# One step of statistics moved from VectorE to TensorE and ScalarE in a kernel that normalises, shifts and blurs images

## What is computed

```
out = displace(group_norm(x, groups of 12 channels, eps 1e-5), round(offset))
kern = exp(-(dx*dx + dy*dy) / (2 * 0.5**2)), 3 x 3, made of frac = offset - round(offset), sum 1
result = x + depthwise_conv(out, kern)
```

## Time and profile before

| | us |
|---|---|
| median of 3 runs | 970.71 (970.06 to 973.06) |
| the profiled execution | 969.36 |
| its span in the profile | 967.6 |
| VectorE busy | 871.9 (90%) |
| ScalarE busy | 714.3 (74%) |
| GpSimd busy | 327.9 (34%) |
| TensorE busy | 201.3 (21%) |
| moved by DMA | 403.49 MB, mean 417 GB/s |

### The profile page before, as it was taken

The page is one execution under the profiler, slowest core; times in us unless marked ns, Lnnn a source line. Parts: engine busy times, 40 slices in busy tenths (PEclk is TensorE's granted clock), DMA queues, the critical chain, the costliest instruction groups (busy, mean ns, idle before and its releaser), DMA issues.

```text
span 967.6 us, 3646 instructions
## 1 busy us (share of the span) xinstructions
PE 201.3 (21%) x896; PEld 195.9 (20%) x896; DVE 871.9 (90%) x947; ACT 714.3 (74%) x412; POOL 327.9 (34%) x197
## 2 busy tenths in 40 slices
PE   0321312212122121222202212122122122220220
PEld 0321312212122121222202212112122122220220
DVE  6389899999999999899989999999999979669991
ACT  3998959777597777778677777777768787877730
POOL 4033341434424333333325264162522323123320
DMA  8999999999999999999999999999999999999997
GB/s 362 429 375 429 423 417 430 420 414 430 417 426 429 421 425 420 427 418 428 417 416 418 420 406 415 424 414 425 423 423 420 427 426 429 427 425 421 414 432 321
DMA packets 28234, 403.49 MB, mean 417 GB/s; under 512 B 3506, under 2 KB 3506, under 8 KB 3634
## 3 DMA queue, kind: packets, MB, share of 16 engines
q0 software_dynamic: 27648, 402.67, 99.4%
q1 hardware_dynamic: 562, 0.57, 0.2%
HBM read 201.90 MB, written 201.33 MB: 417 GB/s over the span
## 4 chain that ended last, share of the span: by engine, by line
DMA 45%; DVE 42%; issue 5%; ACT 4%; POOL 3%; SPq 0%; ACTq 0%; DVEq 0%; POOLq 0%
DMA out<-tiles,row_of 36%; DVE tiles L467 15%; DMA tiles<-x,row_of 8%; DVE rowblur L442 7%; DVE tiles L469 7%; DVE rowblur L447 7%; DVE normed L426 4%; POOL tiles L194 3%; ACT unread L259 3%; ACT unread L263 1%; DMA row_of<-rows 0%; DVE scale L381 0%; DVE shift L384 0%; POOL out L199 0%; DVE var_p L371 0%
## 5 line engine op out<-in xcount | busy, mean ns | idle before, releaser
L259 ACT ACTIVATE unread<-tiles 128x4096 uint8<-128x4096 f32 x94 | 339.9, 3616 | 150.4 <-DMA tiles<-x,row_of 149.8
L263 ACT ACTIVATE unread<-tiles,nmean_p 128x4096 uint8<-128x4096 f32 x94 | 348.7, 3709 | 3.0
L194 POOL DMA_INDIRECT tiles<-x,row_of x95 | 152.9, 1609 | 508.2 <-DMA out<-tiles,row_of 504.6
L467 DVE SCALAR_TENSOR_TENSOR tiles<-rowblur,ratio,tiles 128x735 f32<-128x735 f32 (+24 forms) x192 | 300.0, 1562 | 4.6
L233 PE MATMUL mean_ps<-nmean_p,mask 128*128 128x1 f32 x448 | 100.7, 353 | 539.6 <-ACT unread L259 513.0
L199 POOL DMA_INDIRECT out<-tiles,row_of x96 | 173.6, 1808 | 109.9 <-DVE tiles L467 86.4
L233 PEld LDWEIGHTS mean_ps<-nmean_p,mask 128*128 128x128 f32 x448 | 98.0, 330 | 542.2 <-ACT unread L259 515.7
L442 DVE SCALAR_TENSOR_TENSOR rowblur<-normed,ratio 128x784 f32<-128x784 f32 (+14 forms) x96 | 152.2, 1586 | 3.4
L469 DVE TENSOR_TENSOR tiles<-rowblur,tiles 128x784 f32<-128x784 f32 (+14 forms) x96 | 146.5, 1526 | 3.3
L447 DVE SCALAR_TENSOR_TENSOR rowblur<-normed,ratio,rowblur 128x752 f32<-128x752 f32 (+14 forms) x96 | 145.4, 1515 | 3.4
L233 PE MATMUL var_ps<-var_p,mask 128*128 128x1 f32 x448 | 100.7, 353 | 191.2 <-DVE var_p L371 191.2
(11 more groups left out here) (40 smaller groups left out, 28.1 us busy)
## 6 DMA issues: line engine op xcount, KB each, us to landing
out<-tiles,row_of POOLq DMA_INDIRECT x96, 17.6
tiles<-x,row_of POOLq DMA_INDIRECT x95, 14.7
mask<-masks SPq DMA_DIRECT2D x1, 448.0 KB, 3.1
row_of<-rows SPq DMA_DIRECT2D x1, 48.0 KB, 2.8
offs<-offset SPq DMA_DIRECT2D x1, 48.0 KB
plan_sb<-planned SPq DMA_DIRECT2D x1, 0.4 KB
tiles<-x,first_row POOLq DMA_INDIRECT x1
offs_p<-offset SPq DMA_DIRECT2D x1, 0.4 KB
```

The source lines that it names most:

```text
L194: pool.indirect_dma_start(tiles[:, n % SLOTS, :], None, x_rows, bass.IndirectOffsetOnAxis(ap=row_of[:, n:n + 1], axis=0)).then_inc(loaded[ ...
L259: nc.scalar.activation(unread[:], tiles[:, n % SLOTS, :], ACT.Identity, scale=-1.0 / HW, accum_out=nmean_p[:, i % 2, j:j + 1]).then_inc(nm ...
L263: nc.scalar.activation(unread[:], tiles[:, n % SLOTS, :], ACT.Square, bias=nmean_p[:, i % 2, j:j + 1], accum_out=m2_p[:, i % 2, j:j + 1]). ...
L467: ins = nc.vector.scalar_tensor_tensor(y, t, ratio[:, (tap + 1) // 2, p, 1:2], y, ALU.mult, ALU.add)
```

## The change

TensorE sums three times for a unit in place of twice. Next to the 7 masks there are three new ones, the mask of a tile with itself less 12 on the diagonal; with them the first sum over nmean_p gives 12 times the distance of the group's mean from the partition's mean (into apart_ps). The second sum, with the old masks, is that of the means (mean_ps). The third takes 14 products: the squares within partitions (m2_p) and the squared distances (apart2), accumulated into var_ps. ScalarE squares the distances (apart_of_unit, behind the second pass over the unit's last tile), copies the means out of PSUM into SBUF with the factor 1/12, and takes the root with the factor 1/(12 x 4096) (root_of_unit). root_of_unit for unit u stands between the first and the second pass over the first tile of unit u + 1. Before it copies the means it waits until VectorE has normalised the last tile of unit u - 2. VectorE keeps the reciprocal and the scale; spread_of_unit and the shift are gone, and the tile is normalised as (x + nmean) * scale. The offsets are loaded straight into frac.

```diff
-SMALL = 7
+SMALL = 2
...
-        mask = sb("mask", [128, len(PAIRS), 128])
+        mask = sb("mask", [128, len(PAIRS) + UNIT, 128])
...
-        nmean = sb("nmean", [128, UNIT])
-        apart = sb("apart", [128, UNIT])
+        nmean = sb("nmean", [128, 2, UNIT])
         apart2 = sb("apart2", [128, UNIT])
-        var_p = sb("var_p", [128, UNIT])
         std = sb("std", [128, 2, UNIT])
         rstd = sb("rstd", [128, UNIT])
         scale = sb("scale", [128, 2, UNIT])
-        shift = sb("shift", [128, 2, UNIT])
...
+        apart_ps = ctx.enter_context(nc.psum_tensor("apart_ps", [128, 512], f32))
...
-            sp.dma_start(offs[:], offset.unsqueeze(0).broadcast_to([128, NP, 2])).then_inc(tables_in, 16)
+            sp.dma_start(frac[:], offset.unsqueeze(0).broadcast_to([128, NP, 2])).then_inc(tables_in, 16)
...
-            def sum_groups(ps, src):
+            def sums_of(k):
+                return [j for j, kk in PAIRS if kk == k]
+            def mean_groups(ps, src, own):
                 for k in range(UNIT):
-                    from_ = [j for j, kk in PAIRS if kk == k]
-                    for j in from_:
-                        last = nc.tensor.matmul(ps[:, k:k + 1], mask[:, PAIRS.index((j, k)), :], src[:, j:j + 1],
-                                                start=(j == from_[0]), stop=(j == from_[-1]))
+                    for j in sums_of(k):
+                        at = len(PAIRS) + k if own and j == k else PAIRS.index((j, k))
+                        last = nc.tensor.matmul(ps[:, k:k + 1], mask[:, at, :], src[:, j:j + 1],
+                                                start=(j == sums_of(k)[0]), stop=(j == sums_of(k)[-1]))
                 return last
+            def square_groups(ps, within, between):
+                for k in range(UNIT):
+                    for src in (within, between):
+                        for j in sums_of(k):
+                            last = nc.tensor.matmul(ps[:, k:k + 1], mask[:, PAIRS.index((j, k)), :], src[:, j:j + 1],
+                                                    start=(src is within and j == sums_of(k)[0]),
+                                                    stop=(src is between and j == sums_of(k)[-1]))
+                return last
             for u in range(ALL_UNITS):
                 pe.wait_ge(nmean_done, on_scalar(UNIT * u + UNIT - 1))
-                sum_groups(mean_ps, nmean_p[:, u % 2, :]).then_inc(mean_summed, 1)
-                pe.wait_ge(small_done, u * SMALL + 4)
-                sum_groups(var_ps, var_p).then_inc(var_summed, 1)
+                if u:
+                    pe.wait_ge(apart2_done, u)
+                mean_groups(apart_ps, nmean_p[:, u % 2, :], True).then_inc(apart_summed, 1)
+                if u:
+                    pe.wait_ge(nmean_ready, u)
+                mean_groups(mean_ps, nmean_p[:, u % 2, :], False).then_inc(mean_summed, 1)
+                pe.wait_ge(m2_done, on_scalar(UNIT * u + UNIT - 1))
+                pe.wait_ge(apart2_done, u + 1)
+                if u:
+                    pe.wait_ge(std_done, u)
+                square_groups(var_ps, m2_p[:, u % 2, :], apart2).then_inc(var_summed, 1)
         @block.scalar
         def _(act):
-            def sums(n):
+            def mean_of_tile(n):
                 i, j = divmod(n, UNIT)
-                nth = on_scalar(n)
-                if nth > 1:
-                    act.wait_ge(m2_done, nth - 1)
+                if on_scalar(n) > 1:
+                    act.wait_ge(m2_done, on_scalar(n) - 1)
                 act.wait_ge(loaded[n % SLOTS], landed(n))
                 nc.scalar.activation(unread[:], tiles[:, n % SLOTS, :], ACT.Identity, scale=-1.0 / HW,
                                      accum_out=nmean_p[:, i % 2, j:j + 1]).then_inc(nmean_done, 1)
-                act.wait_ge(nmean_done, nth)
+            def squares_of_tile(n):
+                i, j = divmod(n, UNIT)
+                act.wait_ge(nmean_done, on_scalar(n))
                 nc.scalar.activation(unread[:], tiles[:, n % SLOTS, :], ACT.Square, bias=nmean_p[:, i % 2, j:j + 1],
                                      accum_out=m2_p[:, i % 2, j:j + 1]).then_inc(m2_done, 1)
-            def root(u):
+            def apart_of_unit(u):
+                act.wait_ge(apart_summed, u + 1)
+                nc.scalar.activation(apart2[:], apart_ps[:, 0:UNIT], ACT.Square,
+                                     scale=float(HW) ** 0.5 / GROUP).then_inc(apart2_done, 1)
+            def root_of_unit(u):
                 if u > 1:
-                    act.wait_ge(small_done, (u - 2) * SMALL + 5)
+                    act.wait_ge(normed_done, UNIT * (u - 1))
+                act.wait_ge(mean_summed, u + 1)
+                nc.scalar.activation(nmean[:, u % 2, :], mean_ps[:, 0:UNIT], ACT.Identity,
+                                     scale=1.0 / GROUP).then_inc(nmean_ready, 1)
+                if u > 1:
+                    act.wait_ge(small_done, (u - 2) * SMALL + 1)
                 act.wait_ge(var_summed, u + 1)
                 nc.scalar.activation(std[:, u % 2], var_ps[:, 0:UNIT], ACT.Sqrt, bias=eps[:, 0:1],
-                                     scale=1.0 / GROUP).then_inc(std_done, 1)
+                                     scale=1.0 / (GROUP * HW)).then_inc(std_done, 1)
             for n in range(ALL):
                 if n not in BY_VECTOR:
-                    sums(n)
+                    mean_of_tile(n)
                 if n % UNIT == 0 and n:
-                    root(n // UNIT - 1)
-            root(ALL_UNITS - 1)
+                    root_of_unit(n // UNIT - 1)
+                if n not in BY_VECTOR:
+                    squares_of_tile(n)
+                if n % UNIT == UNIT - 1:
+                    apart_of_unit(n // UNIT)
+            root_of_unit(ALL_UNITS - 1)
         @block.vector
         def _(dve):
-            step(nc.vector.tensor_scalar(frac[:], offs[:], FAR, -FAR, ALU.min, ALU.max))
+            step(nc.vector.tensor_scalar(frac[:], frac[:], FAR, -FAR, ALU.min, ALU.max))
...
-            def spread_of_unit(u):
-                par, base = u % 2, u * SMALL
-                dve.wait_ge(mean_summed, u + 1)
-                nc.vector.tensor_scalar(nmean[:], mean_ps[:, 0:UNIT], 1.0 / GROUP, None,
-                                        ALU.mult).then_inc(small_done, 1)
-                dve.wait_ge(small_done, base + 1)
-                nc.vector.tensor_tensor(apart[:], nmean[:], nmean_p[:, par, :], ALU.subtract).then_inc(small_done, 1)
-                dve.wait_ge(small_done, base + 2)
-                nc.vector.tensor_tensor(apart2[:], apart[:], apart[:], ALU.mult).then_inc(small_done, 1)
-                dve.wait_ge(small_done, base + 3)
-                dve.wait_ge(m2_done, on_scalar(UNIT * u + UNIT - 1))
-                nc.vector.scalar_tensor_tensor(var_p[:], m2_p[:, par, :], 1.0 / HW, apart2[:],
-                                               ALU.mult, ALU.add).then_inc(small_done, 1)
             def scale_of_unit(u):
                 par, base, p = u % 2, u * SMALL, ORDER[UNIT * u]
+                dve.wait_ge(nmean_ready, u + 1)
                 dve.wait_ge(std_done, u + 1)
                 nc.vector.reciprocal(rstd[:], std[:, par]).then_inc(small_done, 1)
-                dve.wait_ge(small_done, base + 5)
+                dve.wait_ge(small_done, base + 1)
                 nc.vector.tensor_tensor(scale[:, par, :], rstd[:], middle[:, p:p + UNIT],
-                                        ALU.mult).then_inc(small_done, 1)
-                dve.wait_ge(small_done, base + 6)
-                nc.vector.tensor_tensor(shift[:, par, :], scale[:, par, :], nmean[:],
...
-                                        scale[:, i % 2, j:j + 1], shift[:, i % 2, j:j + 1],
-                                        ALU.mult, ALU.add).then_inc(normed_done, 1)
+                                        nmean[:, i % 2, j:j + 1], scale[:, i % 2, j:j + 1],
+                                        ALU.add, ALU.mult).then_inc(normed_done, 1)
...
-                spread_of_unit(0)
                 scale_of_unit(0)
                 for n in range(ALL):
                     u, j = n // UNIT + 1, n % UNIT
                     row_taps(n, general)
                     column_tap(n, general, 0)
-                    if j == UNIT - 2 and u < ALL_UNITS:
-                        spread_of_unit(u)
                     column_tap(n, general, 1)
                     if j == UNIT - 1 and u < ALL_UNITS:
                         scale_of_unit(u)
-    masks = np.zeros((128, len(PAIRS), 128), np.float32)
+    masks = np.zeros((128, len(PAIRS) + UNIT, 128), np.float32)
...
+    for k in range(UNIT):
+        masks[:, len(PAIRS) + k, :] = masks[:, PAIRS.index((k, k)), :] - GROUP * np.eye(128, dtype=np.float32)
```

More of the change, by code:

```diff
@@ L107, in norm_shift_blur @@
         rowblur = sb("rowblur", [128, H, W + 2])
-        mask = sb("mask", [128, len(PAIRS), 128])
+        mask = sb("mask", [128, len(PAIRS) + UNIT, 128])
```

(4 more changed lines are left out.)

## The result

The changed kernel takes 980.77 us (median of 5, 978.76 to 982.37) against 972.98 us (median of 5) for the kernel before; the ratio is 1.0091, interval 1.0057 to 1.0125. It is 0.9% slower: the side and the size that were forecast. The profiled execution had a span of 980.6 us, 13.0 more than the one of before; the two medians are 7.8 apart, so some 5 us of what these two traces differ by is the spread between executions.

A forecast was written before the change was run, and what follows sets the result against it. The prediction took DMA transfers to bound the kernel, with VectorE running ahead; VectorE's relief counted 0, and late first stores plus masks 7.7 us, so 970.7 + 7.7 = 978.4 us, range 968 to 988.

The forecast's parts named there:

- The rival that VectorE thins the queue: Slightly late stores cost 15 us; VectorE's relief brings 12 back, less 7.7 at the start: 966.4 us; chance 0.09.
- What is removed: Five VectorE instructions a unit, 32 us of VectorE's work; priced at 0 because the full DMA queue covers it.
- What is added: TensorE's sums of 3.15, 3.15 and 6.3 us, two ScalarE instructions of 0.25 us a unit, larger masks costing 0.5 us.
- What is moved: Root between ScalarE's passes: ScalarE stands 4.5 us a unit; at the start tile 9 begins at 124.3 instead of 108.39.
- The queue: At the start, late stores leave the DMA engines dry 8.6 us; 9.1 with masks, taken as 7.7.
- The first hole: At the start, DMA engines dry for 1 us ahead of store 2 and 4.9 us ahead of store 3.
- the doubtful term: Whether the 2.9 us lost today from 60 to 75 us goes (sum 6.2) or stays (9.1); middle taken, 7.7.
- The second hole: Near 157 us, DMA engines dry for 2.7 us ahead of store 10.
- The middle: Where loads pace ScalarE, its 28.05 us cycle fits in a unit's 29.4 us of loads; cost 0.
- The end: Last unit's root late, tiles 92 to 95 5.2 us later; covered by 3 us, without cover up to 2 us.
- The hidden start: Transfers absorb the late first stores; the masks and some 1.5 us remain, 972.5 us; chance 0.25.
- ScalarE as bound: Turns over TensorE cost over 0.5 us more each, so ScalarE's cycle exceeds the loads; some 1000 us; chance 0.12.

The follow-up runs named there:

- e1: Changed kernel with the root and means' copy put back behind the second pass, all units; 972.64 us against 968.37 for the kernel before, ratio 1.0025.
- e2: Changed kernel with the root put back behind the second pass for units 0 to 6 only; 970.41 us against 968.37 for the kernel before, ratio 1.0002.
- e4: Kernel before with five more small VectorE instructions a unit, results unused; 970.91 us against 968.37, ratio 1.0016.
- e3: Changed kernel without TensorE's products over the squared distances, third sum cut to seven products; 970.99 us against 968.37 for the kernel before, ratio 1.0013.
- e6: Kernel before with a third ScalarE pass over the first tile of units 1 to 7, ahead of the root; 977.74 us against 969.4, ratio 1.0081.
- e7: Kernel before with a third ScalarE pass over the first tile of units 16 to 22, ahead of the root; 971.87 us against 969.4, ratio 1.0015.
- e8: Changed kernel with the root behind the second pass and tile 4's sums by VectorE; 970.19 us against 969.4 for the kernel before, ratio 0.9999.
- e9: Kernel before with units 1 and 2 exchanged, so small tiles come first; 972.94 us against 970.16, ratio 1.0013.
- e10: Changed kernel with root behind second pass, tile 4's sums by VectorE, units 1 and 2 exchanged; 970.27 us against 970.16 for the kernel before, ratio 0.9985.

## Why the prediction was right, point by point

**The bound.** The transfers set the time: e1 and e2 take 20 us from VectorE and gain at most 0.6 and 2.5 us, e4 adds 11 us and loses at most 4, and the changed kernel takes 20 us away and loses. The rival that VectorE thins the queue had 12 us for the relief. No run added the full 32 us to VectorE.

**What is removed** was priced at 0, and e1 and e2, which keep VectorE relieved, are no faster than the kernel before. The size of the relief was off: 32 us forecast, 20.3 measured in busy time. The forecast took 0.2 us from start to start; an instruction itself is 0.16, the pauses do not count as busy, and the last small instruction of a group already ran into the long one behind it. It changes no term of the sum. By the Trainium skill, "Perfetto Trace Analysis", section "Identifying the Most-Contended Engine", occupancy would have pointed at VectorE; its other half, to judge DMA by bandwidth, is the one that this trace bears out, with 417 GB/s over the span and 429 in full stretches.

**What is added.** Three sums of TensorE took 12.2 us from M to the root (54.5 to 66.65, with M where the distances' sum begins), forecast 12.7: each group of products begins some 0.15 us before the one ahead of it is over. ScalarE's two instructions are 0.15 and 0.17 us, not 0.25.

**What is moved.** ScalarE's wait is 4.6 us (forecast 4.5), its cycle 27.5 (28.05). Roots of units 0, 1, 2, 3: 39.2, 66.7, 94.2, 121.7, forecast 39.2, 67.2, 95.2, 123.2. Tile 9 starts at 122.8, forecast 124.3. e3 and e6 show both that this lateness is the cause and that it is enough.

**The queue.** The first hole was forecast at 1 + 4.9 us. Measured from 60 to 90 us the changed kernel moves 413, 370, 377, 344, 128 and 383 GB/s, a loss of 5 x (6 x 429 - 2015)/429 = 6.5 us in all. So of the two bounds of the doubtful term, the lower one was nearer: the 2.9 us of slowness in the kernel before are not added on top. Load 10's issue now takes 0.98 us and not 3.12, with VectorE standing idle. The Trainium skill, "SBUF — State Buffer", section "SBUF: two separate sides", would have it so, if VectorE's instructions there hold the port pair, which no row shows; what the traces show is that issues beside an idle VectorE take 0.96 to 0.98 us in the kernels before and after, and those beside a busy one 0.94 to 4.4. In the changed kernel the hole itself hides what the thin queue would have cost. But e4, with the kernel before's order and its store of tile 3 as late (74.76 us), had a short issue of load 10. Its timeline and its stretches are

```profile
60.94 1.09 POOL L196 DMA_INDIRECT tiles<-x,row_of  x1 [6.98 <-DMA out<-tiles,row_of]
```

```profile
60.00:65.00 5.00, 0.00 (x0) 0.00 (x0) 4.93 (x3) 4.97 (x3) 3.48 (x2) 1.00 1.02 426
65.00:70.00 5.00, 0.50 (x3) 0.50 (x3) 4.93 (x3) 4.94 (x5) 1.52 (x1) 1.00 0.99 321
70.00:75.00 5.00, 2.64 (x13) 2.55 (x12) 4.96 (x4) 4.97 (x3) 0.24 (x1) 1.00 1.02 436
```

which is a loss of 15 - 5 x 1183/429 = 1.2 us in place of 2.9. The same sum gives 3.0 us in e7 (issue 3.32 us) and 2.5 in e8 (2.66), but 1.3 in e9 (1.39), 1.4 in e3 (0.98) and 1.6 in e10 (0.98); of these only e7 has the same work and order as the kernel before up to there. So the slow issues go with some 1.5 us of the 2.9, and the rest stays with fast ones. These are single executions, and none was made to test this. The second hole was forecast at 2.7 us near 157, measured 5 x (858 - 580)/429 = 3.2 us from 155 to 165. Over 200 us the sum is 7.5 us, forecast 7.7 with the masks. That the two agree so well is in part luck: 7.7 was the middle between 6.2 and 9.1, taken because no row decided, and the two holes less the 2.9 us of before make 6.5 + 3.2 - 2.9 = 6.8; the rest lies outside the stretches that were forecast.

**The middle** was priced at 0: e2 and e7 agree with it, within 2.9 and 4.1 us. Between 300 and 900 us ScalarE waits 41.8 us for the squares' sums in 20 units, 2.1 us each, and VectorE waits 35.6 us for roots, where it waited 10.9 us before, but GpSimd waits only 1.5 us for VectorE there, so the queue never feels it.

**The end.** The root of unit 31 comes 12.2 us behind the sum that starts it, and store 92 waits 15.8 us for VectorE. The timeline of the changed kernel, and its stretches:

```profile
951.07 0.26 ACT L307 ACTIVATE std<-var_ps,eps 128x3 f32<-128x3 f32 x1 [5.80 <-PE var_ps L246]
...
952.49 0.96 POOL L199 DMA_INDIRECT out<-tiles,row_of  x1 [15.83 <-DVE tiles L488]
```

```profile
950.00:955.00 5.00, 0.97 (x5) 0.88 (x5) 3.35 (x10) 0.26 (x1) 0.96 (x1) 1.00 0.99 423
955.00:960.00 5.00, 0.00 (x0) 0.00 (x0) 4.82 (x10) 0.00 (x0) 1.25 (x2) 1.00 1.00 426
960.00:965.00 5.00, 0.00 (x0) 0.00 (x0) 4.82 (x6) 0.00 (x0) 0.93 (x1) 1.00 1.00 426
```

The rate holds through it. The queue covered the late root, as forecast.

**The rivals.** The hidden start failed: the holes are there in both runs of the changed kernel. ScalarE as bound failed: it is busy 73% and its cycle is 27.5 us. What stays open is a part of the slow stretch of the kernel before between 60 and 75 us. An earlier root (e8) leaves it, and where issues are fast 1.2 to 1.6 of its 2.9 us are left; whether the queue of two transfers makes these was not tested.

## What to carry to other kernels

Where transfers fill the span, count an edit by the stores and loads that it makes late, and do that stage by stage: the same 3.6 us a unit on ScalarE cost nothing that could be told in the middle (e7), where loads pace it, and 0.8% in the start (e6), where ten tiles have landed and it is the one who is late. A step that is put between two long ones to be early makes its own queue wait for everything ahead of it; compare the length of what it waits for with the work that is left in front of it, here 12.2 us against 7.6. Work taken from the busiest engine is worth nothing while another resource is full. Adding work to that engine is a cheap way to find out, but read in its trace how much was really added: here instructions that wait for each other start 0.2 us apart, while the five of e4, which do not, added 0.36 us together.

## What was not expected

Getting the early chain ahead of the kernel before did not pay: e8 starts tile 9 at 104.0 us, 4.4 us earlier than before, for a ratio of 0.9999. Set out by the start of tile 9, the rates of the first 200 us are: 104.0 us and 411 GB/s (e8), 108.4 and 409 (before), 109.3 and 412 (e4), 110.8 and 412 (e3), 111.9 and 408 (e1), 119.2 and 398 (e6), 122.8 and 393 (changed). So up to 3.5 us of lateness hardly count, and 11 to 14 us cost 5 to 7.5 us. That earliness gives nothing is most likely because the slow stretch of 65 to 75 us is there in both; this was not tested. And the rate in the middle differs from execution to execution as much as the whole effect: between 200 and 960 us the profiled executions have 417 to 423 GB/s, 760 x 6/429 = 10.6 us, with no order in which kernel has which. Two single traces could not have placed this loss from the middle; the first 200 us, with 408 to 412 GB/s in the six kernels e1 to e4, e7 and e8 and 393, 393 and 398 in the changed kernel, its repetition and e6, do.
